# Attention pass of a four-layer graph network on one Trainium2 core: an unread product of 512 columns behind each group's transpose is left out

## The reference

```
q = (x @ Wq.T + bq).reshape(n, H, HD)        # H = 8, HD = 16
k = (x @ Wk.T + bk).reshape(n, H, HD)
v = (x @ Wv.T + bv).reshape(n, H, HD)
attn = jnp.einsum('ehd,ehd->eh', q[row], k[col]) / math.sqrt(HD)
attn = (attn + edge_bias) * cut
attn_exp = jnp.exp(attn - jnp.max(attn, axis=0, keepdims=True))
attn_sum = jax.ops.segment_sum(attn_exp, row, num_segments=n)
attn = attn_exp / (attn_sum[row] + 1e-08)
out = jax.ops.segment_sum(attn[:, :, None] * v[col], row, num_segments=n)
```

## Time and profile before

| | us |
|---|---|
| median of three runs | 15013.75 (15009.1 to 15029.12) |
| profiled execution, its time | 15007.94 |
| its span | 15006.1 |
| PE busy in the span | 7250.9 (48%) |
| DVE busy | 7982.7 (53%) |
| POOL busy | 6624.7 (44%) |
| ACT busy | 2322.5 (15%) |

### The profile page before, as it was taken

One profiled execution on the slowest core, in us unless ns is written; L12 is line 12 of the kernel. 1 busy time (PEld: TensorE's weight loads), 2 busy tenths in 40 slices (PEclk: granted clock), 3 DMA queues, 4 the chain that ended last, 5 costly groups with the idle time before them and its releaser, 6 DMA issues. The chain is left out here.

```text
span 15006.1 us, 180023 instructions
## 1 busy us (share of the span) xinstructions
PE 7250.9 (48%) x37569; PEld 5619.2 (37%) x37570; DVE 7982.7 (53%) x21837; ACT 2322.5 (15%) x6049; POOL 6624.7 (44%) x6504
## 2 busy tenths in 40 slices
PE   5444444411000266653889200026665666666569
PEld 4334333311000266652445100025554555555444
DVE  7555555520000388887020699976665666666631
ACT  0101101000000022210010100001213444444300
POOL 0555555567777400001100277765543555555400
PEclk9555555555555555555889655556676888888789
DMA  0000000010000266664658466666672222222347
GB/s 26 1 1 1 1 1 1 1 31 1 10 18 18 75 201 199 196 187 143 245 215 306 138 203 202 204 178 201 206 189 73 82 83 83 83 82 83 64 165 264
DMA packets 1114463, 1673.21 MB, mean 112 GB/s; under 512 B 287476, under 2 KB 828112, under 8 KB 1075632
## 3 DMA queue, kind: packets, MB, share of 16 engines
q1 hardware_dynamic: 543264, 1032.94, 20.7%
q0 software_dynamic: 234960, 339.86, 9.0%
q10 hardware_dynamic: 335808, 296.39, 6.7%
HBM read 1263.13 MB, written 405.27 MB: 111 GB/s over the span
## 5 line engine op out<-in xcount | busy, mean ns | idle before, releaser
L1317 POOL DMA_INDIRECT big<-tab_h,idx x1664 | 1832.1, 1101 | 2159.2 <-DMA tab_h<-asrc 1293.5
L2145 POOL DMA_INDIRECT big<-tab_kv,idx x1664 | 1592.5, 957 | 1380.9 <-PE banks L2220 488.8
L898 POOL DMA_INDIRECT by_src<-big,h x1568 | 1508.2, 962 | 1198.5 <-DVE h L620 748.7
L1194 DVE SCALAR_TENSOR_TENSOR acc<-acc,h,banks 128x128 f32<-128x128 f32 x3966 | 1082.1, 343 | 1343.6 <-remote 1108.8
L898 POOL DMA_INDIRECT by_dst<-x,h x1456 | 1547.6, 1063 | 496.8 <-issue 462.6
L1419 DVE SCALAR_TENSOR_TENSOR acc<-big,room,acc 128x1280 f32<-128x1280 f32 (+1 forms) x960 | 1378.9, 1525 | 21.6 <-DMA big<-cells 21.6
L1085 PE MATMUL banks<-we2t,idx 128*128 128x8 f32 x3328 | 762.2, 358 | 958.6 <-issue 457.2
L1085 PEld LDWEIGHTS banks<-we2t,idx 128*128 128x128 f32 x3328 | 753.0, 331 | 992.6 <-issue 786.1
L1659 PE MATMUL banks<-big,h 128*128 128x448 f32 x2744 | 1060.3, 547 | 94.6 <-issue 77.7
L2220 PE MATMUL banks<-big,room 128*128 128x136 f32 x3328 | 694.8, 342 | 680.3 <-DVE acc L2317 647.4
L898 POOL DMA_INDIRECT by_dst<-room x112 | 107.2, 957 | 1990.6 <-POOLq L2439 1956.7
(11 more groups left out here) (467 smaller groups left out, 13973.6 us busy)
## 6 DMA issues: line engine op xcount, KB each, us to landing
big<-cells SPq DMA_DIRECT2D x262, 1568.0 KB
cells<-acc SPq DMA_DIRECT2D x1985, 64.0 KB
cells<-acc ACTq DMA_DIRECT2D x1984, 64.0 KB
big<-cells ACTq DMA_DIRECT2D x196, 640.0 KB
head_rows<-big SPq DMA_DIRECT2D x416, 264.0 KB
big<-head_rows SPq DMA_DIRECT2D x208, 528.0 KB
acc<-w_rows SPq DMA_DIRECT2D x208, 512.0 KB
big<-loc_rows SPq DMA_DIRECT2D x208, 256.0 KB
```

The costliest lines, as they stand in the source:

```text
L898: pool.indirect_dma_start(self.target, bass.IndirectOffsetOnAxis(self.slots[:, t:t + 1], axis=0), self.rec[:, t, :], None).then_inc(self.s ...
L1194: dve.scalar_tensor_tensor(k.cells[:, c * SIDE + m, :], before, k.cell_flag[:, bass.ds(j * (2 * SUB) + s * SUB + c * SIDE + m, 1)], cell_b ...
L1317: pool.indirect_dma_start(k.stage[:, m % BODY, :], None, k.tab_h_dram, bass.IndirectOffsetOnAxis(k.idx[:, m:m + 1], axis=0)).then_inc(k.ga ...
L2145: pool.indirect_dma_start(far[:, m % (G * RING), 0:2 * C], None, k.tab_kv_dram, bass.IndirectOffsetOnAxis(k.idx[:, m:m + 1], axis=0)).then ...
```

## The change

`idle` and its place in TensorE's list of stages are removed, with the view of the ramp that it read. The other stages keep their order and their lags, and no other engine's list is touched.

```diff
-    idle_rows = k.ramp_pair[:, :, :].rearrange("p c i -> p (c i)").unsqueeze(1).to_broadcast([P, 2, 2 * P])
...
                 ins.then_inc(matched, 1)
 
-            def idle(g, i, j):
-
-                pe.matmul(k.psum[3][:, :].rearrange("p (a c) -> p a c", a=2), k.ident_bf[:, :], idle_rows,
-                          start=True, stop=True)
-            turns(pe, [(10, multiply), (2, look), (0, turn), (2, idle), (4, at_group(3, flip)),
+            turns(pe, [(10, multiply), (2, look), (0, turn), (4, at_group(3, flip)),
                        (5, at_group(3, spread_top))])
```

## The result

| | kernel before | changed kernel |
|---|---|---|
| median, us | 15011.42 (15002.81 to 15029.12, 4 runs) | 15490.11 (15463.47 to 15518.87, 4 runs) |
| profiled span, us | 15006.1 | 15461.7 |
| DVE busy, us | 7982.7 | 7966.9 |
| PE busy, us | 7250.9 | 7183.9 |

The change is slower: 1.0316 times the kernel before, 95% interval 1.0301 to 1.0331, or 479 us. The forecast was 21 us faster. Nearly all of it lies in the attention pass: from the first to the last record of the multiply line it takes 2732 us before (11467.2 to 14199.5) and 3175 us after (11477.6 to 14652.8), 443 us more, of a span that grew by 456 us.

A forecast was written before the change was run, and what follows sets the result against it. The attention pass was taken as paced by VectorE, its busy time plus its own sequencer's stops, with TensorE beside it. Product -44 and clock +23 gave -21 us: about 14993 us for the median, range 14950 to 15040 us.

The forecast's parts named there:

- the reading of VectorE's stops: Attention pass, VectorE at L2239: 144.7 us per 1000 under a false DMA name, taken for VectorE's own sequencer handing out nothing.
- the prediction's own example: A 4.02 us wait at L2239: the look it reads had long ended, so VectorE seemingly had nothing to wait for.
- the 39.4 us for which TensorE is named: Attention pass, per 1000 us: VectorE's waits attributed to TensorE, 53 of them, taken as all that lay on the path.
- the sign itself: Changed profile: VectorE's stops changing in number or length would mean they hang on TensorE's program and the prediction was wrong.
- TensorE's program gets shorter ... so nothing: TensorE's turn: one matmul fewer shifts where its sequencer fetches; TensorE has slack there, so the cost is zero.
- The product's time, -44 us: TensorE in the attention pass: 147 VectorE waits for TensorE each shrink by 0.30 us; ends 0 and -109 us.
- 105 + 58 waits in 303 groups: TensorE's waits for VectorE's add and ScalarE's one-hots per 1000 us, read as absorbing the saved time in two of three groups.
- The clock, +23 us: TensorE's clock in the pass falls from 0.82 to 0.75: 147 waits x 1.1 us x upper-level share falling 0.64 to 0.50.
- the nearest relative: The GAT layer's weighted pass, the same kind of loop without such a product, with a granted clock of 0.70.
- The swallowed gain: Rival, attention pass: VectorE's stops of 3 to 6 us absorb what was gained; result 0, 15014 us; chance 0.20.
- the larger gain: Rival, attention pass: TensorE's lateness is removed rather than shortened; -44 to -109 us, 14905 to 14970 us; chance 0.13.
- The clock case: Rival, attention pass: TensorE's clock falls below 0.69, its late arrivals lengthen; up to +59 us, 15073 us; chance 0.15.

## Why the prediction was wrong

**The step that failed** is the reading of VectorE's stops: "I take it for its own sequencer". The signs were right in one point (nothing that L2239 reads was late by its own records, and the DMA was a false name) and the conclusion was not. TensorE's look had ended, but its semaphore update had not arrived. In the prediction's own example the look ended at 12400.50, its update stands in the trace at 12405.04, and VectorE starts at 12405.06. Of the 203.7 us at L2239 in the earlier trace rows only the 59.0 on "issue" have no late update behind them; they are one stop of 3 us per round and stay at 49 to 76 us per 1000 in the traces shown here. The 144.7 us are such late updates wherever they could be followed, and they vanish when the gathers or the condition do. So the pass was not paced by VectorE with TensorE beside it. All four engines wait for each other in a ring: GpSimd's gathers go on, TensorE's updates wait, the others stop, and the ring restarts when they arrive. How often it stops hangs on small things in TensorE's program. The same step left 26.0 us in 10 waits at L2270 out of the 39.4 us for which TensorE is named. The prediction named the sign itself ("VectorE's stops changing in number or length, which would mean that they hang on TensorE's program after all") and gave it no chance.

**"TensorE's program gets shorter ... so nothing"** failed with it. That was costed at zero and is where the 479 us are: with one matmul of 8 columns left in each turn they are gone. The changed profile agrees. TensorE's wait for the add was to grow beyond 234 us per 1000 and fell to 127.5, and a group takes 3.91 us and not 3.30.

**The product's time, -44 us.** No run shows this gain. It can't be seen under the stops. Away from them, moving the product out of the way of the small products at a kept length gave 0.9978 and 0.9968, some 25 to 37 us, with an interval that ends at or near 1 each time. That is another edit in the other condition, and it would fit the size. Taking the product away there gave nothing clear of noise: 0.9988 (0.9967 to 1.0009) with 8 columns left and 1.0024 (0.9998 to 1.005) with none in the loop. The step to it was also worded too strongly: 105 + 58 waits in 303 groups are a little over half of the groups, not two of three.

**The clock, +23 us.** 0.75 was forecast and 0.70 came, the value of the nearest relative in the earlier trace rows; the choice above it was too hopeful. By the prediction's own formula 0.70 costs 147 x 1.1 x (0.64 - 0.40) = 39 us. Without the stops and at the same place in the turn, behind the small products, the median round gives 2.52 us per group with 512 columns (clock 0.94) and 2.57 with 8 (clock 0.84), a difference of 0.045 x 832 = 37 us, which has the clock in it. So the price was of the right order and never that of the result. At 0.70 the prediction's own terms give -44 + 39 = -5 us, and at 0.50 they give +59; the loss was 479. The changed pass stood at 0.70 to 0.72 with two transposes in every turn, beside multiply and look, and did not fall toward the 0.50 of the prediction's bound. The Trainium skill ("TensorE: Matmul & The Clock Gate", "Part 4: PE-mode transpose") says that a transpose does not count as activity in the way a matmul does. No run here separates the two kinds, so this neither confirms nor refutes it.

**The rivals.** The swallowed gain and the larger gain did not come. The clock case had the right sign, by another mechanism. It had a chance of 0.15, of which 0.11 beyond the noise; its longest case reached 15073 us, and the range ended at 15040.

**What stays open.** Why four small products per batch keep the rounds short, and one does not, is not settled. The order of instructions does not explain it, nor the streamed columns, nor the clock; the number in the loop's body fits the two runs that could tell, three of four turns were never run with the stops, and a shift of the body's place was only run where the stops were absent. What makes the condition itself, why TensorE's updates come late in it when there are gathers, and whether issuing or transfers do it, was not found. The product of 512 columns behind the small products was never run with the stops, so whether it beats the kernel before in both conditions is open too.

## What to carry to other kernels

When every engine stops at once for some us and the releaser named is a transfer that has no business there, compare the start of the stopped instruction with the end of its true producer on the other engines: two consumers that start together, long after both producers ended, point to the producer's semaphore updates and not to the consumer. A loop in which the engines wait for each other under such stops can fall into longer rounds by an edit that costs nothing by any sum, so an instruction whose result is unread may still hold a schedule; compare the lengths of the single rounds, not only their mean. And measure the pair again elsewhere: here one edit measured 1.032, 1.006 and 1.032, and the nearest edit to it 1.0024 (0.9998 to 1.005) where the stops were absent.

## What was unexpected of the hardware

- The kernel before took 14981 us (median) on one occasion and 11593 us on another, on the same chip. In the condition with the stops 540 to 709 of some 60,000 register and semaphore instructions of a trace last 0.68 to 0.72 us, in the other none or one.
- TensorE's semaphore updates arrived up to 7.2 us after the end of their instruction, in order, and then several within 0.2 us, while GpSimd issued gathers of 0.95 us each with 0.30 us between. Without gathers such stops were gone in the same condition: 2.54 against 3.91 us per group in the change beside it.
- Rounds of the changed kernel in its first trace: 26 of 49 over 62 us, most of them at 66.0 to 66.3, 18 between 57 and 62, and 5 under 57.
